# Four graph layers on one core: the output biases of layers 0 and 3 moved from TensorE products to GpSimd and VectorE additions, with all orders written anew

## What is computed

```python
# layer 0: attention without projections on layernorm(h), then an MLP
x = x + out
y = layer_norm(x, gamma2, beta2)
mlp = jax.nn.gelu(y @ W1 + b1, approximate=False) @ W2 + b2
return x + mlp
# layer 3: attention with projections, bias behind the output projection
out = out @ Wo + bo
return jax.nn.relu(out)
```

## Time and profile before

| | |
|---|---|
| runs shown | 4241.14, 4243.43 and 4238.12 us, median 4241.14 us |
| profiled execution | 4241.92 us, its span 4240.1 us, mean granted TensorE clock 0.988 |
| busy over the span | PE 95%, DVE 76%, ACT 51%, POOL 10% |
| chain that ended last | PE 90%, DVE 5%, ACT 4% |

### The profile page before, as it was taken

How to read it: one execution, slowest core, us unless ns; L and a number is a source line. 1 busy time by engine, 2 the same in 40 slices (tenths; PEclk the granted TensorE clock), 3 DMA queues, 4 the chain that set the end, 5 groups by cost and what they waited for, 6 DMA issues and landing times.

```text
span 4240.1 us, 58963 instructions
## 1 busy us (share of the span) xinstructions
PE 4042.6 (95%) x22884; PEld 1929.7 (46%) x22884; DVE 3223.4 (76%) x6473; ACT 2166.5 (51%) x3361; POOL 408.3 (10%) x469
## 2 busy tenths in 40 slices
PE   5799999999999999999999999999999999999997
PEld 1344444444444444444444444444444444444443
DVE  5677778877778877777877777877778877788854
ACT  3454555544555554555544555544555544555532
POOL 0001011101011101110100110100110100110100
PEclk9999999999999999999999999999999999999998
DMA  3111111111111111111111111112111111211000
GB/s 99 29 42 50 56 37 49 34 53 51 56 36 51 31 53 52 56 36 51 31 52 54 56 35 51 31 51 56 56 32 54 31 51 56 56 31 46 21 31 31
DMA packets 212311, 193.90 MB, mean 46 GB/s; under 512 B 144448, under 2 KB 179008, under 8 KB 203584
## 3 DMA queue, kind: packets, MB, share of 16 engines
q1 hardware_dynamic: 212032, 190.12, 15.3%
HBM read 138.95 MB, written 17.56 MB: 37 GB/s over the span
## 4 chain that ended last, share of the span: by engine, by line
PE 90%; DVE 5%; ACT 4%; DMA 1%; issue 1%; SPq 0%; POOL 0%; POOLq 0%; ACTq 0%; DVEq 0%
PE O L477 12%; PE M L425 11%; PE M L438 10%; PE S L358 6%; PE S L524 6%; PE O L371 6%; PE M L491 6%; PE O L540 6%; PE M L449 6%; PE O L481 5%; PE M L502 3%; PE M L416 3%; PE M L582 3%; PE O L382 2%; ACT PP L625 2%; PE M L398 2%
## 5 line engine op out<-in xcount | busy, mean ns | idle before, releaser
L1014 DVE SCALAR_TENSOR_TENSOR PG<-g,tcg,mT 128x512 f32<-128x512 f32 x1024 | 691.2, 742 | 33.1 <-PE O L481 21.4
L625 ACT ACTIVATE PP<-S,reach 128x1024 f32<-128x1024 f32 x512 | 542.6, 1111 | 318.8 <-PE O L371 114.5
L906 DVE TENSOR_TENSOR PP<-PP,mT 128x1024 f32<-128x1024 f32 x512 | 597.3, 1218 | 16.5 <-ACT PP L625 16.0
L477 PE MATMUL O<-PG,V 128*32 128x512 f32 x4096 | 550.9, 602 | 18.5 <-DVE PG L1014 17.0
L425 PE MATMUL M<-hT,W 128*128 128x512 f32 x1024 | 460.6, 603 | 3.1 <-ACT hT L660 2.8
L438 PE MATMUL M<-W,H 128*128 128x256 f32 x2048 | 459.7, 378 | 0.0
L438 PEld LDWEIGHTS M<-W,H 128*128 128x128 f32 x2048 | 377.3, 189 | 71.7 <-issue 10.6
L1126 POOL TENSOR_SCALAR ve<-mv 128x4 f32<-128x4 f32 x192 | 97.8, 509 | 3197.4 <-DVE mv L864 3197.4
L358 PE MATMUL S<-hT 32*128 32x512 f32 x2048 | 301.3, 658 | 30.8 <-ACT PP L625 29.4
L739 ACT ACTIVATE PP<-S,sh 128x1024 f32<-128x1024 f32 x256 | 272.1, 1118 | 87.5 <-DVE Q L916 49.0
L603 ACT ACTIVATE V<-z,nb,rs 128x256 f32<-128x256 f32 x128 | 76.6, 602 | 467.4 <-DVE nb L896 467.4
(11 more groups left out here) (136 smaller groups left out, 5608.5 us busy)
## 6 DMA issues: line engine op xcount, KB each, us to landing
g<-t_rows SPq DMA_DIRECT2D x64, 1024.0 KB, 4.7
adj<-adj_in SPq DMA_DIRECT2D x32, 1024.0 KB, 5.5
x<-x_in SPq DMA_DIRECT2D x32, 512.0 KB, 4.0
z<-t_rows SPq DMA_DIRECT2D x64, 256.0 KB, 4.0
out<-x SPq DMA_DIRECT2D x32, 512.0 KB, 2.9
W<-w_in SPq DMA_DIRECT2D x1, 3072.0 KB, 13.0
mT<-z SPq DMA_TRANSPOSE x128, 2.5
m<-V SPq DMA_TRANSPOSE x128, 2.5
```

The source lines that it names most:

```text
L477: e.matmul(k.O[0][r:r + 32, :], s.V[:, jt, 64 * hh + 32 * v:64 * hh + 32 * v + 32], p[:, u, :], start=(jt == 0), stop=(jt == NT - 1))
L625: e.activation(p[:, 2 * pair:2 * pair + 2, :], k.S[:, 2 * pair:2 * pair + 2, :], ACT.Exp, bias=k.reach[:, 7:8], scale=SC0).then_inc(k.e0.s ...
L906: e.tensor_tensor(p[:, 2 * pair:2 * pair + 2, :], p[:, 2 * pair:2 * pair + 2, :], s.mT[:, jt:jt + 1, :].to_broadcast([128, 2, N]), ALU.mul ...
L1014: e.scalar_tensor_tensor(out=p[:, u, :], in0=s.T[hh], scalar=s.tcg[:, 1, hh, jt:jt + 1], in1=s.mT[:, jt, :], op0=ALU.max, op1=ALU.mult).th ...
```

## The change

TensorE no longer forms the bias products: the product of a tile starts with its first true matmul. GpSimd gets two steps for each batch. `xb` adds b2 to x of all four tiles (128x1024) once the first layer norm has been read from x, and VectorE's `resid0` waits for it. `xo` subtracts the negated bias (`nbo`, minus bo and minus bv times Wo) from x once the layer norm of layer 3 has been read. VectorE's `wo` now writes max(M, nbo) into hT, and a new step `xz` adds hT to x for all four tiles. Since max(M, nbo) - nbo is max(M + bias, 0), the result is the same. ACT's `qt(b, q)`, which writes hT, now waits for `xz` of the batch three before. The preparation of the bf16 parts of the biases is gone.

```diff
@@ Pe.w2
-        self.wait_ge(k.b_ready, 2)
-        e.matmul(k.M[t % 2][:, 0:256], k.onesb[:, :], k.bias["b2"][:, :], start=True, stop=False)
...
-                         start=False, stop=(kk == 7))
+                         start=(kk == 0), stop=(kk == 7))
@@ Pe.wo
-        self.take(f"M{tp}", k.woa.at(b, tp))
-        self.wait_ge(k.b_ready, 2)
+        self.take(f"M{tp}", k.mo.at(b, tp))
         for t in (2 * tp, 2 * tp + 1):
-            e.matmul(k.M[tp][:, 256 * (t % 2):256 * (t % 2) + 256], k.onesb[:, :], k.bias["bo"][:, :],
-                     start=True, stop=False)
@@ Act.qt
         if b >= NS:
-            self.wait_ge(*k.wo.at(b - NS, 1))
+            self.wait_ge(*k.woa.at(b - NS, 0))
@@ Dve.resid0
+        self.wait_ge(*k.xb.at(b, 0))
@@ Dve.wo and Dve.xz
-        xx = s.x[:, 2 * tp:2 * tp + 2, :]
-        e.scalar_tensor_tensor(out=xx, in0=k.M[tp][:, :].rearrange("p (t d) -> p t d", t=2), scalar=0.0, in1=xx, op0=ALU.max, op1=ALU.add).then_inc(k.woa.sem, 1)
+        self.wait_ge(k.bvo_read, 1)
+        e.tensor_tensor(s.hT[:, :, 256 * tp:256 * tp + 256], k.M[tp][:, :].rearrange("p (t d) -> p t d", t=2),
+                        k.nbo[:, None, :].to_broadcast([128, 2, D]), ALU.max).then_inc(k.mo.sem, 1)
+
+    @step
+    def xz(self, b):
+        e, k, s = self.e, self.k, self.k.of(b)
+        self.wait_ge(*k.mo.at(b, 1))
+        self.wait_ge(*k.xo.at(b, 0))
+        xx = s.x[:, :, :].rearrange("p (c i) d -> p c i d", c=2)
+        e.tensor_tensor(xx, xx, s.hT[:, :, :].rearrange("p i (c d) -> p c i d", c=2), ALU.add).then_inc(k.woa.sem, 1)
@@ Pool
+    def xb(self, b):
...
+        self.wait_ge(*k.z0.at(b, 3))
+        e.tensor_tensor(s.x[:, :, :], s.x[:, :, :], k.b2[:, None, :].to_broadcast([128, NT, D]),
+                        ALU.add).then_inc(k.xb.sem, 1)
...
+    def xo(self, b):
...
+        self.wait_ge(k.bvo_read, 1)
+        self.wait_ge(*k.zr[3].at(b, 3))
+        e.tensor_tensor(s.x[:, :, :], s.x[:, :, :], k.nbo[:, None, :].to_broadcast([128, NT, D]),
+                        ALU.subtract).then_inc(k.xo.sem, 1)
@@ gpsimd_program
+        do.gmax(b3, 1)
+        do.xb(b2)
+        do.rs(b4, 5)
+        do.xo(b4)
+        do.rs(b3, 4)
+        do.rs(b2, 2)
+        do.gmax(b3, 2)
```

More of the change, by code:

```diff
@@ L822, in prep_b @@
             self.wait_ge(k.reached, 1)
[L823 to L840, removed]
+            e.scalar_tensor_tensor(out=k.nbo[:, :], in0=k.M[0][:, 0:256], scalar=-1.0, in1=k.w("bo"), op0=ALU.mult,
+                                   op1=ALU.subtract).then_inc(k.bvo_read, 1)
     @step
@@ L1327, in tensor_program @@
         do.sc3(b3, 2)
+        do.b2r(b1, 0, 2)
+        do.pv3(b3, 1)
+        do.b2r(b1, 0, 3)
+        do.pj(b2, 2, 0)
+        do.pj(b2, 2, 1)
+        do.sc3(b3, 3)
+        do.pj(b2, 2, 2)
+        do.pj(b2, 2, 3)
+        do.dn3(b3, 0)
+        do.pv3(b3, 2)
+        do.prep_b(b1)
+        do.tt(b1, 0, 0)
+        do.tt(b1, 0, 1)
+        do.pv3(b3, 3)
+        do.w1(b1, 0)
+        do.w1(b1, 1)
+        do.grow(b2, 2)
+        do.dn3(b3, 1)
+        do.w1(b1, 2)
+        do.w1(b1, 3)
+        do.w1(b1, 4)
+        do.w1(b1, 5)
+        do.w1(b1, 6)
+        do.w1(b1, 7)
+        do.w2(b1, 0)
+        do.w2(b1, 1)
+        do.w2(b1, 2)
+        do.w2(b1, 3)
 def scalar_program(do):
@@ L1539, in vector_program @@
         do.bag(b2, 4, 3)
-        do.bag(b0, 0, 0)
-        do.bst(b0, 0, 1)
-        do.sc0(b1, 4)
-        do.sc0(b1, 5)
-        do.nb(b2, 4)
+        do.sc0(b1, 5)
+        do.pa0(b1, 2)
+        do.sq3(b3, 0)
+        do.sc0(b1, 6)
+        do.nb(b2, 4)
+        do.sq3(b3, 1)
+        do.sc0(b1, 7)
+        do.pa0(b1, 3)
+        do.sh3(b3)
+        do.zb(b1)
+        do.sc3(b3, 0)
+        do.rc(b1, 0, 0)
+        do.b2r(b1, 0, 0)
+        do.rc(b1, 0, 1)
+        do.bag(b0, 0, 0)
+        do.fin(b1, 0, 0)
@@ new lines, in vector_program @@
+        do.sc3(b3, 1)
+        do.bst(b1, 2, 0)
+        do.pa3(b3, 0)
+        do.b2r(b1, 0, 1)
+        do.bag(b1, 2, 0)
+        do.rc(b1, 0, 2)
+        do.b2r(b1, 0, 2)
+        do.fin(b1, 0, 1)
+        do.fin(b1, 0, 2)
+        do.bst(b1, 2, 1)
+        do.rc(b1, 0, 3)
+        do.bag(b1, 2, 1)
+        do.b2r(b1, 0, 3)
+        do.bst(b1, 2, 2)
+        do.fin(b1, 0, 3)
+        do.pa3(b3, 1)
+        do.bag(b1, 2, 2)
+        do.bst(b1, 2, 3)
+        do.bag(b1, 2, 3)
+        do.pj(b2, 2, 0)
@@ L1545, in vector_program @@
+        do.pj(b2, 2, 1)
+        do.sc3(b3, 2)
+        do.pj(b2, 2, 2)
+        do.nb(b1, 2)
+        do.prep_b(b1)
+        do.prep_w(b1)
         do.bst(b0, 0, 2)
         do.bag(b0, 0, 1)
-        do.pa0(b1, 2)
+        do.pj(b2, 2, 3)
+        do.gmax(b2, 2)
+        do.sc3(b3, 3)
+        do.gprep(b2, 2)
+        do.pa3(b3, 2)
+        do.pa3(b3, 3)
+        do.masks(b0, 0)
+        do.bst(b0, 0, 3)
         do.bag(b0, 0, 2)
-        do.bst(b0, 0, 3)
-        do.sq3(b3, 0)
-        do.sc0(b1, 6)
@@ L1575, in gpsimd_program @@
-def gpsimd_program(do):
-    for it in range(1, NB + 4):
-        b1, b2, b3, b4 = it - 1, it - 2, it - 3, it - 4
+        do.resid0(b1)
+        do.nb(b0, 0)
+        do.w2(b1, 0)
+        do.masks(b0, 1)
+        do.bst(b0, 1, 0)
+        do.gvals(b2, 2)
+        do.bag(b0, 1, 0)
+        do.bst(b1, 3, 0)
+        do.w2(b1, 1)
+        do.gw(b2, 2, 0)
+        do.bag(b1, 3, 0)
+        do.w2(b1, 2)
+        do.bst(b1, 3, 1)
+        do.bst(b0, 1, 1)
+        do.bst(b1, 3, 2)
+        do.bst(b0, 1, 2)
```

297 lines of the change are left out of this document (112 added, 185 removed).

## The result

The changed kernel takes 4277.3 us (median of 4 runs, 4269.9 to 4281.49) against 4239.74 us for the kernel before, measured beside it (4 runs): ratio 1.0084, interval 1.0072 to 1.0096, some 37 us slower. Forecast were 4331 us, 90 more. The sign is right, the size is more than twice too large.

What follows compares the result with a forecast made beforehand. TensorE's work was taken to set about 102 us of each turn, VectorE's about 26; 0.3 + 0.8 + 2.1 = +3.2 us per turn over 28 turns, +90 us on 4241.14, gave 4331 us, range 4205 to 4375.

Steps and rivals of the forecast that it cites:

- Products, -0.87 us per turn: Eight bias matmuls per batch leave TensorE, 0.109 us each, all in the part of the turn that TensorE leads.
- `xz`, +1.14 us: One added 128x1024 addition in VectorE's always-busy stretch between `wo` and `pa0`; nothing hides its 1.14 us per turn.
- The same 1.14 us and not a second cost: `qt` comes later behind the added addition, but the first `gpv` waits for VectorE anyway, so no further cost.
- The order, "I take 0": Rest of the permuted instruction order: 0 us per turn, bounds -0.3 and +0.7; some steps come nearer, some farther.
- GpSimd's additions, +2.9 us per turn: `xb` and `xo` hold VectorE's two-SBUF-input instructions: +0.8 us at `diag` before `wo`'s second half, +2.1 us at `sc0`'s masking.
- gets in before the next one: GpSimd stands still until VectorE's two-SBUF-input instruction ends, then starts before VectorE's next; seen on a 128x4 instruction.
- No exclusion: Rival: VectorE goes on while GpSimd adds; +0.3 us per turn, 4249 us (4241 to 4269); 23% with about the same time.
- Faster by the new order: Rival: permuted lists take at least 1.14 us of waiting out of VectorE's stretch; only products count, 4213 us, 25%.
- The wait moves elsewhere: Rival: `xb` or a later `gmax` holds `nb` or `gprep`, a few tenths of a us per turn; no own chance.
- the turn (131 us): Sign in the changed profile: a steady turn of about 131 us instead of 127.6.
- the held masking (3 us): Sign: a VectorE instruction beside `xo`, the masking of `sc0`, is late or lasts some 3 us in place of 1.22.

## Why the prediction was right in sign and wrong in size

**Products, -0.87 us per turn: nearly right.** 24.4 us were measured where 32 x 0.87 = 28 were forecast, and 0.77 us for a turn.

**`xz`, +1.14 us: right on VectorE, but it is not all.** From the second half of `wo` to the end of `pa0` VectorE needs 2724.64 - 2700.06 = 24.58 us, 23.46 before (2679.52 to 2702.98): 1.12 more. Removing `xz` however gives 45.7 us, 14 more than 28 x 1.14, and 46.7 in the old order. Where the 14 lie is only in part known. Without `xz` the matmuls of `qt` take 8.1 us less in all (47.0 for 55.1), at a mean clock of 0.987 in place of 0.972, and the kernel that keeps TensorE busy in the gap has that clock again and is 6 us faster, which is not clear of noise. So the clock is a likely part, and by that kernel not the larger one, though its added transposes may hide some of it; the rest was not taken apart. "The same 1.14 us and not a second cost" was wrong: TensorE waits earlier and longer, at `qt`, and its clock falls behind that gap.

**The order, "I take 0": too low, within its bounds.** It costs 12 us, 0.46 us per turn, where the bounds were -0.3 and +0.7. A new wait stands in a place that the prediction listed (`gmax` of layer 2 behind later statistics) and priced at tenths: 0.77 us in each of 30 turns, 23.2 us in all, more than the order costs.

**GpSimd's additions, +2.9 us per turn: the step that failed.** Measured are 12 us in all, 0.4 per turn (0.32 by the profiled turns). The prediction held that exclusion, shown by a four-column instruction that "gets in before the next one", lets a long addition in as well: "`xo` [...] gets in at the end of one of them and holds the next: +2.1 us". Exclusion is real; the getting in is not. The long addition found no way in between VectorE's back-to-back instructions with two SBUF inputs in any profile read here (7.26 us in the turn shown of the change, 6.85 in the old order, for 2.35 us of work). It waits for a VectorE instruction that reads PSUM, and its work begins beside such instructions. What it then holds is only its own overhang over those instructions: 11 us in the changed order, 40 in the old one. `xb` was taken to hold `diag` for 0.8 us; a change of code of 7.34 us, not 6.00, put it beside `wo`'s second half and `b2r`, and in the turn shown it holds one `fin` by 0.22 us (0.64 in place of 0.42).

The rule of the Trainium skill that I leant on (SBUF — State Buffer, Who interferes with whom) is borne out in its exclusion: in the experiment in the old order `xo` makes no way beside the masking, and `fin` none beside `xo`. The prediction read "whichever comes first" as if `xo`, once ready, went ahead of VectorE's next instruction. There the runs decide: with VectorE's queue full it is GpSimd that waits. The estimate of 2.25 us for 1024 columns, from the figure that the Trainium skill gives for 2048 (GPSIMD Engine Reference, Elementwise — side-by-side cycle accounting), agrees with the 2.35 us measured.

**The sum.** By the parts that were measured alone the loss is -24 (products) + 12 (order) + 46 (`xz` with the clock) + 12 (additions) = 46 us. Measured are 37; by the turns it is -0.77 + 0.46 + 1.47 + 0.32 = 1.48 us against 1.29. Each was taken out of or put into another kernel, so waits that lie side by side may be counted twice, and each difference has some us of noise; this was not settled. Two errors partly made up for each other: 81 us (28 x 2.9) for GpSimd in place of 12, and 32 (28 x 1.14) for `xz` and the order in place of 58.

**The rivals.** *No exclusion* gave 4249 us, too little, since it had `xz` and the order too cheap, and the held instructions speak against it. Yet what the prediction named as its sign came true: VectorE's four maskings kept their pace while `xo` ran (4.62 us). It could not tell "no exclusion" from "GpSimd is the one that waits". *Faster by the new order* has the wrong sign: the order alone is slower. *The wait moves elsewhere*, which I had priced at tenths inside another case, is the order's 0.46 us per turn, about a third of the loss. Of the signs that were named, the turn (131 us) came at 128.96 and the held masking (3 us) at 2.68 us for two of them, where 2.35 is the undisturbed value. PE's busy time fell by 12 us and not by 28, and PE's longer waits came at `qt` and `grow`, not at `sc0` and the first `gpv`.

## What to carry to other kernels

In these runs a long GpSimd addition cost VectorE only what it overhung into an instruction with two SBUF inputs: look for its start in VectorE's timeline, count the PSUM readers from there, and move it until they cover it. Eight products of 0.11 us on a full TensorE are cheap against an extra 1.14 us on an engine that leads for a fifth of the turn; the version that moves b2 alone and adds nothing to VectorE is the fastest complete kernel here (4224.9 us). And an extra instruction is to be priced with the gap that it opens on TensorE: `xz` cost 14 us more than its own time, in both orders, and the granted clock was lower with it.

## What the runs showed of the hardware

- A 128x1024 addition of two SBUF inputs on GpSimd takes 2.33 to 2.38 us in the changed kernel as `xb`, mostly beside VectorE's PSUM readers or its rest, and 6.5 us in the mean at `xo`'s place, nearly all of it waiting while VectorE works on two SBUF inputs.
- A four-column GpSimd instruction does get in between two such VectorE instructions. Why a long one doesn't isn't shown, nor whether an instruction with one SBUF input would let it in.
- A write of 128x2048 on GpSimd takes 1.8 us beside them and holds none, but it holds VectorE's small TENSOR_SCALAR instructions on SBUF (182 and 168 ns) until its own end, up to 1448 and 1373 ns.
- GpSimd's change of code costs on both ways: 5.7 to 6.5 us ahead of `gmax`, 6.6 to 7.8 us from `gmax` to an addition; the prediction took 6.00 for both. Ahead of the write of zeros behind `gmax` no such time stood in the timeline: `gmax` began at 2657.38 and took 0.39 us, the write began at 2657.65.
- Behind TensorE's two gaps of 0.52 and 1.15 us the granted clock was 0.79 in the mean of the next 8 us, and eight matmuls took 1.99 in place of 1.14 us.
